# A low-rank stack written by DMA to rows eight partitions apart, in place of 48 neighbouring partitions

## The reference, cut to what matters

```python
xn = layernorm(x)                                  # x: 2048 rows of 512
s  = s4_convolution(xn)                            # a state-space kernel of 512 taps, plus D * xn
def lora(x, w, a, b):                              # a has 16 rows: rank 16
    return x @ w.T + 2.0 * (x @ a.T) @ b.T
h1, h3 = lora(xn, w1, A1, B1), lora(xn, w3, A3, B3)   # 512 -> 1376
g = silu(lora(silu(h1) * h3, w2, A2, B2))             # 1376 -> 512
out = x + s * g
```

## Time and profile before

| what | us |
|---|---|
| median of 3 runs | 433.69 (432.15 to 433.96) |
| the profiled execution, its own time | 434.08 |
| its span | 432.3 |
| PE busy | 420.8 (97% of the span) |
| DVE, ACT, POOL busy | 160.9, 102.6, 65.0 |

### The profile page before, as it was taken

The page is one execution under the profiler, slowest core; times in us unless marked ns, Lnnn a source line. Parts: engine busy times, 40 slices in busy tenths (PEclk is TensorE's granted clock), DMA queues, the critical chain, the costliest instruction groups (busy, mean ns, idle before and its releaser), DMA issues.

```text
span 432.3 us, 5022 instructions
## 1 busy us (share of the span) xinstructions
PE 420.8 (97%) x1868; PEld 342.4 (79%) x1868; DVE 160.9 (37%) x245; ACT 102.6 (24%) x168; POOL 65.0 (15%) x128
## 2 busy tenths in 40 slices
PE   7969999999999999999999999999999999999995
PEld 7947888888778888888778888888778888888773
DVE  4636776655557322222315322223314211111115
ACT  5524432333314111211212211221212111111111
POOL 3226452531150101400000001400000000000000
PEclk9999999999999999999999999999999999999999
DMA  8493653221043411000003310000002000000002
GB/s 265 114 170 113 213 192 95 78 89 47 19 148 111 147 34 49 0 2 0 2 0 125 121 46 20 29 0 0 0 0 98 0 0 0 0 0 0 0 0 97
DMA packets 14063, 26.19 MB, mean 61 GB/s; under 512 B 2480, under 2 KB 4208, under 8 KB 14032
## 3 DMA queue, kind: packets, MB, share of 16 engines
q1 hardware_dynamic: 13888, 25.41, 19.9%
q0 software_dynamic: 160, 0.59, 0.4%
HBM read 20.37 MB, written 4.53 MB: 58 GB/s over the span
## 4 chain that ended last, share of the span: by engine, by line
PE 91%; DMA 3%; DVE 2%; SPq 1%; ACT 1%; issue 1%; POOL 0%; DVEq 0%; ACTq 0%
PE h L781 19%; PE h L782 19%; PE h L783 19%; PE f L783 9%; PE f L781 9%; PE f L782 9%; PE spare L768 2%; DMA lora_stack<-lora_spread_split 2%; DVE w L624 1%; DMA lora_first<-lora_dram 1%; SPq L458 1%; PE spare L783 1%; PE spare L781 1%; PE spare L782 1%; PE f L776 0%
## 5 line engine op out<-in xcount | busy, mean ns | idle before, releaser
L781 PE MATMUL h<-xt,w 128*128 (+4 forms) x356 | 139.4, 391 | 0.2 <-DVE w L624 0.2
L783 PE MATMUL h<-xt,w 128*128 (+4 forms) x356 | 138.3, 388 | 0.0
L782 PE MATMUL h<-xt,w 128*128 (+4 forms) x356 | 138.2, 388 | 0.0
L781 PEld LDWEIGHTS h<-xt,w 128*128 128x128 f32 (+1 forms) x356 | 66.5, 187 | 15.7 <-DVE w L624 0.6
L783 PEld LDWEIGHTS h<-xt,w 128*128 128x128 f32 (+1 forms) x356 | 66.3, 186 | 15.1
L782 PEld LDWEIGHTS h<-xt,w 128*128 128x128 f32 (+1 forms) x356 | 66.5, 187 | 14.6
L660 DVE TENSOR_TENSOR g<-g,h 128x512 f32<-128x512 f32 (+1 forms) x44 | 30.3, 688 | 127.4 <-PE h L783 127.4
L665 DVE TENSOR_TENSOR ghl<-g,ghl 128x512 fp32r<-128x512 f32 (+1 forms) x44 | 31.9, 725 | 100.9 <-ACT ghl L520 100.8
L783 PE MATMUL f<-ghl,w2f 128*128 128x512 f32 (+1 forms) x176 | 69.5, 395 | 0.0
L781 PE MATMUL f<-ghl,w2f 128*128 128x512 f32 (+1 forms) x176 | 69.4, 395 | 0.0
L782 PE MATMUL f<-ghl,w2f 128*128 128x512 f32 (+1 forms) x176 | 69.2, 393 | 0.0
(11 more groups left out here) (103 smaller groups left out, 274.9 us busy)
## 6 DMA issues: line engine op xcount, KB each, us to landing
raw<-w_dram SPq DMA_DIRECT2D x28, 256.0 KB, 3.8
xres<-xT_dram SPq DMA_DIRECT2D x4, 1024.0 KB, 7.3
outT_dram<-xres SPq DMA_DIRECT2D x16, 256.0 KB, 2.4
rows_next<-x_dram SPq DMA_DIRECT2D x4, 512.0 KB, 3.8
scale_rows<-scales_scratch SPq DMA_DIRECT2D x3, 512.0 KB, 3.9
xn<-x_dram SPq DMA_DIRECT2D x4, 256.0 KB, 4.3
rows<-x_dram SPq DMA_DIRECT2D x2, 512.0 KB, 7.0
raw<-w_dram SPq DMA_DIRECT2D x4, 224.0 KB, 2.5
```

The costliest lines, as they stand in the source:

```text
L781: pe.matmul(out, w[1], m[0], start=start, stop=False)
L782: pe.matmul(out, w[0], m[1], start=False, stop=False)
L783: return pe.matmul(out, w[0], m[0], start=False, stop=stop)
```

## The change

The 16 rows of each of the three groups no longer lie next to each other. Group n (0, 1, 2) takes the partitions n, n + 8, n + 16, ... n + 120. The rows of the three groups together are partitions 0, 1, 2, 8, 9, 10, 16, ... The source, the columns, the number of DMAs, their sizes and their order stay, and so do the two instructions that zero the tile. Nothing else is changed.

```diff
 STACK = ((1, 0), (0, 1), (0, 0))
+STACK_STEP = P // R
...
             for n, (st, mv) in enumerate(STACK):
                 for hl, cols, lane_cols in ((st, slice(0, ST_COLS), slice(0, LANES_ST)),
                                             (mv, slice(ST_COLS, LORA_COLS), slice(LANES_ST, LANES_ST + LANES_MV))):
-                    sync.dma_start(lst[n * R:(n + 1) * R, cols].bitcast(F32).rearrange("r (k c) -> r k c", k=P // R),
+                    sync.dma_start(lst[n:P:STACK_STEP, cols].bitcast(F32).rearrange("r (k c) -> r k c", k=P // R),
                                    spread_hl[:, hl, lane_cols].bitcast(F32)).then_inc(stack_in, 16)
```

## The result

| | us |
|---|---|
| changed kernel, median of 4 runs | 428.71 (428.17 to 429.46) |
| kernel before, median of 4 runs | 432.99 (432.15 to 433.96) |
| ratio | 0.989, 95% interval 0.9869 to 0.991 |
| profiled execution of the changed kernel, its span | 428.78, 427.0 |

The kernel became 1.1% faster, 0.9 to 1.3% by the interval. Three later groups of runs gave the changed kernel 428.85, 428.53 and 428.38 us against 434.04, 433.76 and 433.93 before, with ratios of 0.9882 to 0.9889. The forecast was 428.7.

The account below looks back on a forecast made before the run. PE, busy for 97% of the span, was taken as the bound, with its longest wait on the slowly written stack. 3.6 + 1.8 - 0.4 = 5.0 us off the median 433.69 gave 428.7 us, range 427.4 to 431.6.

Parts of the forecast that it names:

- What bounds the kernel: Whole span: PE is busy for 97%; whatever PE wins before 45 us reaches the end unless a new wait comes.
- The rate: Stack DMAs: writing rises from 107 to 215 GB/s, so the data take 5.1 us in place of 10.2.
- the sign named: Sixth stack DMA: it should land in about 3.3 us after issue and not in 8.46.
- the threshold of 163 GB/s: Stack writing: from about this rate on, data are through in 6.7 us and PE's wait is gone.
- Term 1: PE's wait for the DMAs that fill the stack, ending at 30.70, goes away: 3.6 us gained.
- Term 2: Fold (1, 2) to the next folds: PE's clock stays at the upper level, 3.25 us for 5.03: 1.8 us gained.
- The pause of 0.8 us ahead of the small matmuls: At 23.49 in the kernel before: taken as evidence that shorter pauses leave PE's clock at 1.00.
- Term 3: DVE's low part at about 31 us meets POOL's long operations: 0.4 us lost, between 0 and 1.0.
- B: Stack reads and writes share capacity; it lands at 28.0, PE waits 1.0: 429.7 or 431.5 us; chance 0.14.
- C: Stack rate stays 107 GB/s, or the gain is given back at DVE or POOL behind 36 us: 433.7; chance 0.12.
- D: Source and target overlap stalls writes, stack goes in below 107 GB/s: slower, 438.6 us at 72 GB/s; chance 0.04.

Follow-up runs that it names:

- measured alone: Kernel before, with 14 matmuls of 512 columns in the fast operand format on PE ahead of its wait for the stack: 432.05 us, ratio 0.9967.

## Why the prediction was right, step by step

**What bounds the kernel** held. PE's time behind 45 us stayed as it was, and the lead of 5.60 us at the folds of 43.13 was still there at the fold of 114.83 (109.23 after). Of it 5.3 us reach the end of the profiled span. Most of the missing 0.3 us lies at one matmul at the start of block 1. In the chains of the kernel before and of the changed kernel it is this one:

```profile
133.56 0.28 PE h L781
```

```profile
128.02 0.52 PE h L782
```

In another execution of the changed kernel (step8b) the same matmul, at 127.95, took 0.27. So 0.24 us of it are a difference between single executions, and not of the change.

**The rate** was put at 215 GB/s and came out at 202 to 205. The sixth DMA took 4.2 us to landing where the sign named was 3.3, and landed near 26.2 and not at 25.5. The lower rate makes 0.3 us of this (1.09 MB at 203 GB/s are 5.4 us and not 5.1); the rest was not followed. PE came at 26.55 + 0.39 = 26.94, so the margin was about 0.7 us and not 1.5. The term was hidden either way. The run with rows 3 apart shows what lies on the other side of the threshold of 163 GB/s: at the 127 to 132 GB/s of its rows above PE waits 2.5 us, loses the clock too, and more than half of the gain is gone.

**Term 1**, the wait: 3.6 forecast, 3.76 read from the two chains, 0.1 of it because the changed kernel's earlier part ran that much ahead.

**Term 2**, the clock: 1.8 forecast, 5.61 - 3.76 = 1.85 in the chains, and some 1.4 when it was measured alone. The two do not differ beyond the noise: the interval of the second is 0.9 to 1.9 us, and in the chains of that run the part from fold to folds is shorter by 5.03 - 3.30 = 1.73 us. One reading in its support was wrong. The pause of 0.8 us ahead of the small matmuls is one between weight loads; PE's own record has no idle time there (3.00 of 3.00 us from 22 to 25 in the kernel before). So these rows could not say that a short standstill leaves the clock alone.

**Term 3**, DVE and POOL meeting in another order: 0.4 lost was forecast, and it is the step that failed. The low part of (1, 2) did grow, from 1.46 to 1.72, as POOL's first operation lay over its start, and it ended 2.4 us after PE's product (2.6 had been worked out). POOL's first operation comes first here, then the lines of DVE:

```profile
30.72 1.28 POOL L953 TENSOR_TENSOR den_im<-den_im,res 128x512 f32<-128x512 f32 x1 [5.01 <-ACT res L554]
30.23 0.69 DVE L661 TENSOR_TENSOR g<-g,h 128x512 f32<-128x512 f32 x1 [2.09 <-PE h L784]
30.83 1.72 DVE L625 TENSOR_TENSOR w<-raw,w 128x512 fp32r<-128x512 f32 x1
...
34.20 0.92 DVE L625 TENSOR_TENSOR w<-raw,w 128x512 fp32r<-128x512 f32 x1
35.27 1.55 DVE L666 TENSOR_TENSOR ghl<-g,ghl 128x512 fp32r<-128x512 f32 x1 [0.15 <-ACT ghl L521]
```

But the two DVE operations behind it met less of POOL. They took 0.92 and 1.55, and in the kernel before they had taken longer:

```profile
39.56 1.16 DVE L624 TENSOR_TENSOR w<-raw,w 128x512 fp32r<-128x512 f32 x1
40.65 1.78 DVE L665 TENSOR_TENSOR ghl<-g,ghl 128x512 fp32r<-128x512 f32 x1
```

From the folds at 30.12 to the folds at 37.53 there are 7.41 us, and 7.40 before: nothing was lost. The forecast followed the first collision through and not the whole row of them.

That the whole time came out to the digit is luck. Term by term the forecast was 5.0 and the lead 5.3 to 5.6; it was taken from a median of 433.69, while the median of the kernel before was 432.99 beside the result and 433.76 to 434.04 in the later groups.

**The rivals.** B (target rows among the source rows cost rate): the target rows 2 apart lie mostly outside the eight source partitions, those 8 apart within them, and both land in 4.1 to 4.2 us; no cost of the overlap shows. C and D would have needed a rate of 107 or less, or a new wait behind 36 us; the page shows neither.

## What to carry to other kernels

When DMA engines are full and move a quarter of what they move elsewhere, look at the partitions that one transfer writes, and deal its rows out evenly over the groups of four neighbours (a group and the one 32 further on counted as one); the range spanned is not what matters, rows 2 apart did as well as 8 apart. A wait of PE costs more than its length when the clock falls behind it: here 3.6 us of standing still took about 1.4 us more with it, and filler matmuls alone, in the fast format and no longer than the wait, win that back. When a wait goes, ask what is next: PE's margin was 0.7 us, and work moved out of its way came back as a wait elsewhere until its owner was changed.

## What the runs showed of the hardware that was not expected

PE can be busy and yet lose its clock. In the run with 32-bit filler matmuls on operands of 16 partitions PE's record shows no idle time, and the granted clock falls from the upper to the lower level (1.2 GHz). It stays there until the filler ends at 46.9, some 16 us, and for about 4.5 us of matmuls in the fast format behind it:

```profile
26.00:30.00 4.00, 4.00 (x12) 1.90 (x11) 0.29 (x1) 0.60 (x1) 0.00 (x0) 1.00 1.08 120
30.00:34.00 4.00, 4.00 (x8) 1.51 (x7) 0.00 (x0) 0.00 (x0) 0.00 (x0) 0.62 0.92 346
34.00:38.00 4.00, 4.00 (x6) 1.55 (x5) 0.00 (x0) 0.00 (x0) 0.00 (x0) 0.50 0.00 0
...
46.00:50.00 4.00, 4.00 (x12) 2.70 (x11) 0.69 (x1) 1.23 (x3) 0.00 (x0) 0.50 0.00 0
50.00:54.00 4.00, 4.00 (x19) 3.36 (x18) 1.47 (x2) 1.24 (x3) 2.52 (x3) 0.82 0.00 0
```

Whether the format or the 16 partitions do it was not tried. A standstill of 2.5 us ahead of the stack went with the loss of the clock with rows 3 apart. A shorter one can be enough, it seems: in some executions, two of them of the changed kernel itself, PE waits 1.5 to 1.7 us for ACT from 7.5 us on (`PE f L777 <- ACT xn L525`), and the granted clock falls about there too and is 0.50 until 11 us or later. What set it off was not tried, and the 2.5 us are no limit that these runs show. Rows 7 apart were written at 240 GB/s from 22.5 to 24.5 us, with the DMA share at 1.03, a fifth more than rows 8 apart (202).
